# Building the graph's cell matrices with one-hots of one chunk between additions, and the gated unit's products in three rounded ones

## The chip, the cores and the metric

The program runs on one core of one Trainium2 chip. The number that counts is the device time of one execution in microseconds (us), median of several runs. The kernel is written engine by engine: TensorE (PE, with its weight loads PEld), VectorE (DVE), ScalarE (ACT), GpSimd (POOL) and SyncE (SP, which issues most of the DMAs) each have an instruction stream of their own, and they wait for each other only where the program says so, by semaphores.

## The reference

Four graph layers in a row over 1250 nodes of 512 values and 21250 edges. Each layer takes `h = relu(layernorm(x))` and adds its result to x:

```python
deg = max(segment_sum(1, dst), 1)
x = x + L0(h, ...)    # mean of the neighbours' rows, two linear maps, layernorm
x = x + L1(h, ...)    # two weighted graph convolutions, rows divided by their norm
x = x + L2(h, ...)    # messages and a gated unit, below
x = x + L3(h, ...)    # sum of the neighbours' rows by edge_weight1, one linear map

def L2(h, src, dst, edge_attr, ...):
    m = relu(concat(h[src], edge_attr) @ W1.T + b1) @ W2.T + b2
    agg = segment_sum(m, dst)
    i_r, i_z, i_n = split(agg @ W_ih.T + b_ih)
    h_r, h_z, h_n = split(h @ W_hh.T + b_hh)
    r, z = sigmoid(i_r + h_r), sigmoid(i_z + h_z)
    n = tanh(i_n + r * h_n)
    h_new = (1 - z) * n + z * h
    return h + gamma * (h_new - run_mean) * rsqrt(run_var + eps) + beta
```

Everything is float32.

## The kernel before

The 1250 nodes are 10 tiles of 128 (NT = 10), a row of 512 is 4 blocks of 128 (KT = 4). The stages, with their place in the profiled execution in us:

- **Sorting (0 to 297).** The edges are sorted on the chip by their cell (tile of the target, tile of the source: 100 cells of 128x128) into chunks of 128 edges with one cell each, 272 chunks (CELL_CHUNKS), and in a second order by target for layer 2. Indirect DMAs of POOL write the sorted records to memory. Beside it PE turns and folds the weights.
- **Building (297 to 540).** Each chunk of 128 edges becomes a part of three matrices (edge count, edge_weight, edge_weight1) over its cell. ACT makes the one-hot of the sources (`one_hot_sources`, abs at L847 and relu at L852). DVE makes the one-hot of the targets (`hots`, L1560: the row of numbers `iota1` compared with each edge's number, two chunks in one instruction, 128x256). POOL multiplies it by the two weights (`weights_turn`, L725, two chunks in one instruction, 128x512). PE multiplies the sources' one-hot with the three targets' one-hots (L1142, 128x384) into one of four banks of PSUM, and DVE adds the bank to the cell's place in SBUF (`add_block`, L1576). That place comes from a table: a TENSOR_LOAD (L1565) takes 8 places into registers of DVE's sequencer at the start of each turn of 8 chunks (TURN). The one-hots have 8 slots each. An addition waits for the one before it, as two may go to the same cell. POOL also issues one of layer 2's 168 scatters (L717) in each turn, 32 of them in this stage (EARLY = 4 groups of COL = 8).
- **Layers 0 and 1 (540 to 838).** Products with these matrices. POOL does the other 136 scatters, then clears `g` at L760 once layer 1 is done, and then waits for the first gathers.
- **Messages (838 to 1149).** For 184 chunks of 128 edges, POOL gathers rows (L784) and copies their indices four chunks at a time (L771), PE, DVE and ACT make the messages and add them up by target. SP loads the gated unit's six 512x512 matrices in 48 pieces between its other loads: 4 ahead of the loop, 4 in each turn of 16 chunks, 4 behind it.
- **The gated unit (1149 to 1372).** For each tile t, PE turns the tiles of h and of the sums by `turn_tile` (L1046; one tile ahead), ACT copies them to SBUF, and PE makes four results by `linear` (L1060): r and z with 8 blocks each, hn and in with 4 each. All of it is float32 by float32; the profile shows each such matmul as two records, so a tile has 24 matmuls and 48 records. DVE reads the banks and computes the gates from L1743 to L1769 with ACT's sigmoid, tanh and square root between; the batch-norm's factors are made once at L1723 to L1726, ahead of the first tile.
- **Layer 3 (1372 to 1487).** The sum over neighbours with three rounded products: each operand is the sum of a high part, rounded to fp32r by a copy on ACT (L992, L997), and a low part, the rest, made by a subtraction on DVE (L1732, L1737); PE adds high by high, high by low and low by high (L1328).

The four banks `pb[4..7]` go round over all of DVE's jobs in the order of a list (V), and a job may only be begun when the fourth before it has been read:

```python
def to_dve(job):
    at_least(pe, dve_read, V[job] - 3)
    return dve_bank(job)
```

## Time and profile before

| | |
|---|---|
| median of 3 runs | 1490.85 us (1489.72 to 1490.96) |
| the profiled execution | 1488.92 us, span 1486.7 us |
| mean granted clock of TensorE | 0.957 |
| PE busy | 1309.6 us, 88% of the span |
| DVE busy | 988.1 us, 66% |
| POOL busy | 719.2 us, 48% |
| PEld busy | 685.9 us, 46% |
| ACT busy | 565.0 us, 38% |
| of the chain that ended last: PE | 45% |
| issue (waiting for nothing shown) | 17% |
| POOL | 14% |
| DMA | 13% |
| DVE | 9% |

The span runs from the first to the last instruction; the execution's own time is 2.2 us longer. Busy shares are means over stages with different limits: PE is busy nearly throughout, but a matmul that PE could have made sooner counts as busy all the same. The clock granted to TensorE is 2.4 GHz at 1.00 and 1.2 GHz at 0.50. So each stage has to be read for itself, by the distance from one step to the next on the engine that is never free.

### The profile page before, as it was taken

How to read it: one execution, taken by the hardware profiler on the slowest of the kernel's cores; microseconds unless marked ns; L12 is line 12 of the kernel's file. 1: busy time of each engine (PE TensorE's matmuls, PEld its weight loads, DVE VectorE, ACT ScalarE, POOL GpSimd, SP SyncE). 2: the span in 40 equal slices, each digit the busy share in tenths (PEclk: the TensorE clock that was granted, in tenths of full speed). 3: DMA queues.
4: the chain of work that ended last, by engine and by line, in shares of the span. 5: the costliest groups of instructions: out<-in, count | busy, mean ns of one | idle time of the engine just before them, and what ended most of it. 6: DMA issues, size and time to landing. Idle time of an engine off the chain costs nothing.

```text
span 1486.7 us, 19898 instructions
## 1 busy us (share of the span) xinstructions
PE 1309.6 (88%) x4184; PEld 685.9 (46%) x4184; DVE 988.1 (66%) x1719; ACT 565.0 (38%) x1438; POOL 719.2 (48%) x873
## 2 busy tenths in 40 slices
PE   5859898098888888959998899999998999997998
PEld 2534443043333333438874444444454444443775
DVE  8798253078888889841286388888896576667432
ACT  0211311066666620121011388888886221222210
POOL 0677777677777725766771266676663000000000
PEclk9989999599999999979999999999999999998999
DMA  8832522110000044443223577777775000000220
GB/s 337 322 118 65 191 66 79 46 57 18 19 21 16 9 181 156 121 154 96 89 81 127 161 224 215 228 227 225 227 221 184 20 1 0 1 0 18 71 89 34
DMA packets 87236, 167.86 MB, mean 113 GB/s; under 512 B 16108, under 2 KB 44654, under 8 KB 84628
## 3 DMA queue, kind: packets, MB, share of 16 engines
q1 hardware_dynamic: 59044, 102.19, 20.4%
q0 software_dynamic: 25472, 59.97, 13.2%
q10 hardware_dynamic: 2672, 5.11, 1.1%
q8 instruction: 24, 0.39, 0.1%
q14 instruction: 24, 0.20, 0.0%
HBM read 115.97 MB, written 51.25 MB: 112 GB/s over the span
## 4 chain that ended last, share of the span: by engine, by line
PE 45%; issue 17%; POOL 14%; DMA 13%; DVE 9%; POOLq 1%; ACT 1%; DVEq 1%; ACTq 0%
PE pb L1060 21%; DMA arena<-p_rows,gidx 11%; POOL cell_rows L671 8%; PE pb L1142 6%; PE pb L1168 6%; PE pb L1328 5%; PE pb L1176 2%; POOL tiles L725 2%; PE pb L1046 1%; POOL arena L725 1%; PE pb L1083 1%; PE pb L1258 1%; DMA cell_rows<-tiles,gidx 1%; DVE arena L1560 1%; POOL arena L784 1%
## 5 line engine op out<-in xcount | busy, mean ns | idle before, releaser
L784 POOL DMA_INDIRECT arena<-p_rows,gidx x184 | 191.5, 1041 | 67.3 <-issue 58.4
L717 POOL DMA_INDIRECT dst_rows<-ering,gidx x168 | 172.2, 1025 | 100.0 <-issue 71.4
L671 POOL DMA_INDIRECT cell_rows<-tiles,gidx x168 | 168.8, 1004 | 68.0 <-issue 39.7
L1258 PE MATMUL pb<-arena 128*128 128x512 f32 x368 | 191.6, 604 | 5.6 <-ACT arena L944 5.6
L1576 DVE TENSOR_TENSOR arena<-pb,arena 128x384 f32 x272 | 150.0, 552 | 45.8 <-PE pb L1142 24.4
L1060 PE MATMUL pb<-ws,tiles 128*128 128x512 f32 (+1 forms) x360 | 146.3, 554 | 12.0 <-ACT tiles L806 12.0
L1684 DVE TENSOR_TENSOR arena<-pb,arena 128x512 f32<-128x512 f32 x184 | 124.4, 686 | 41.6 <-DMA arena<-p_rows,gidx 39.5
L1142 PE MATMUL pb<-arena 128*128 128x384 f32 x272 | 107.5, 520 | 47.9 <-POOL arena L725 46.1
L847 ACT ACTIVATE arena<-iota,free 128x128 f32<-128x128 f32 x272 | 94.3, 393 | 123.4 <-PE pb L1142 82.4
L1142 PE MATMUL pb<-tiles,arena 128*128 128x384 f32 x272 | 106.2, 514 | 22.8 <-POOL tiles L725 21.0
L1060 PE MATMUL pb<-arena,tiles 128*128 128x512 f32 x240 | 103.9, 593 | 0.0
L1060 PE MATMUL pb<-arena 128*128 128x512 f32 x240 | 103.8, 592 | 0.0
L1274 PE MATMUL pb<-high,low 128*128 128x512 f32 x138 | 93.7, 679 | 7.7 <-DVE arena L1699 6.3
L1060 PEld LDWEIGHTS pb<-ws,tiles 128*128 128x128 f32 x360 | 66.6, 193 | 69.0 <-issue 53.6
L1691 DVE SCALAR_TENSOR_TENSOR low<-arena,high 128x512 fp32r<-128x512 f32 x138 | 94.4, 684 | 4.4 <-ACT high L951 2.2
L951 ACT ACTIVATE high<-arena 128x512 fp32r<-128x512 f32 x138 | 86.1, 624 | 25.7 <-DVE arena L1684 21.7
L1142 PEld LDWEIGHTS pb<-arena 128*128 128x128 f32 x272 | 42.2, 192 | 113.1 <-ACT arena L852 85.3
L1168 PE MATMUL pb<-arena 128*128 128x256 f32 x400 | 88.2, 380 | 2.0 <-DVE arena L1649 1.5
L725 POOL TENSOR_TENSOR arena<-arena,free 128x512 f32<-128x512 f32 x68 | 70.8, 1042 | 35.8 <-DVE arena L1560 32.4
L1168 PEld LDWEIGHTS pb<-arena 128*128 128x128 f32 x400 | 75.8, 190 | 16.0 <-issue 3.3
L1328 PE MATMUL pb<-parts 128*128 128x512 f32 x300 | 75.2, 409 | 8.3 <-DVE parts L1737 8.2
L1176 PE MATMUL pb<-ws,arena 128*128 128x512 f32 x160 | 73.6, 616 | 9.5 <-DVE tiles L1620 7.0
(258 smaller groups left out, 2129.8 us busy)
## 6 DMA issues: line engine op xcount, KB each, us to landing
dst_rows<-arena SPq DMA_DIRECT2D x6, 2046.0 KB, 17.5
ering<-in_edge_attr_dram SPq DMA_DIRECT2D x41, 256.0 KB, 3.0
arena<-adj SPq DMA_DIRECT2D x10, 640.0 KB, 3.8
arena<-dst_rows SPq DMA_DIRECT2D x24, 264.0 KB
arena<-wt_gru SPq DMA_DIRECT2D x48, 128.0 KB
ws<-dst_rows SPq DMA_DIRECT2D x22, 264.0 KB, 2.9
arena<-in_x_dram SPq DMA_DIRECT2D x18, 256.0 KB, 8.7
arena<-in_L_gnn_W_hh_dram SPq DMA_DIRECT2D x3, 1024.0 KB
```

The costliest lines, as they stand in the source:

```text
L671: nc.gpsimd.indirect_dma_start(cell_rows[:, :], bass.IndirectOffsetOnAxis(gidx[:, SPAN * a + k:SPAN * a + k + 1], 0), cring[:, a, k], None ...
L717: nc.gpsimd.indirect_dma_start(dst_rows[:, :], bass.IndirectOffsetOnAxis(gidx[:, k:k + 1], 0), ering[:, k, :], None).then_inc(e_scattered[ ...
L725: nc.gpsimd.tensor_tensor(hot[:, :, 1:3], hot[:, :, 0:1].to_broadcast([P, 2, 2, P]), cellm[:, bass.ds(TURN * i + 2 * q, 2), 2:4].unsqueeze ...
L784: nc.gpsimd.indirect_dma_start(rows[:, k, :], None, p_rows[:, :], bass.IndirectOffsetOnAxis(gidx[:, k:k + 1], 0)).then_inc(g_landed[k], 16)
L1060: ins = nc.tensor.matmul(b[:, 0:wide], x[:, k], w[:, k], start=m == 0, stop=m == n - 1)
L1142: nc.tensor.matmul(pb[k % 4][:, 0:3 * P], ohs[:, k], ohd(k, 1).rearrange("p a m d -> p (a m d)"), start=True, stop=True).then_inc(block_do ...
L1168: ins = nc.tensor.matmul(b[:, 0:wide], blocks_of[:, s], rows_of[:, s, 0:wide], start=s == 0, stop=s == NT - 1)
L1176: ins = nc.tensor.matmul(b[:], matrix(0, t)[:, s], ws[:, s // KT, s % KT] if s < 2 * KT else h[:, s], start=s == 0, stop=s == NT - 1)
L1258: nc.tensor.matmul(e_bank(k)[:], erowT[:, k % 4], w1e_sb, start=True, stop=True).then_inc(edge_mm, 1)
L1328: ins = nc.tensor.matmul(b[:], a3[:, t % 2, left, k], h3[:, right, k], start=k == 0 and left + right == 0, stop=k == NT - 1 and left == 1)
L1576: vtt(cell, pb[k % 4][:, 0:3 * P].rearrange("p (m d) -> p m d", m=3), cell, ALU.add).then_inc(block_added, 1)
L1684: vtt(row, e_bank(k)[:], row, ALU.add).then_inc(msg_added, 1)
```

## The change

Two parts, made together.

**Building.** DVE makes the one-hot of one chunk (128x128) between every two additions, 8 chunks ahead, rather than of two chunks at every second; the row of numbers it compares with lies in PSUM (`counting`, a copy of `iota1` in `pb[4]`). POOL weights four chunks in one instruction (HALF = 4, 128x1024). DVE's turn is 16 chunks; of the places it loads 1 at its start and 3 more after each third addition. A scatter goes out every 16 chunks, so 16 lie in this stage (EARLY = 2) and 152 behind it.

**The gated unit.** Its operands are split as in layer 3. At its start ACT rounds the 24 blocks of the six matrices (`high_of_weights`) and DVE makes their low parts (`low_of_weights`). For each tile the high part is copied by ACT out of the bank in which PE turned it, and the low part made there by DVE (`low_of_turned`), for h and for the sums; there is one set of these parts, written anew for each tile. A result is three fp32r products for each block. PE first does the parts of r, z and hn that come from h, then the parts of r, z and in that come from the sums, and DVE reads hn, r, z, in. The batch-norm's factors come behind the weights' low parts. The pieces of the matrices are loaded 8 ahead of the message loop and none behind it; layer 3's first matrices and its weight are loaded when hn of the last tile is there.

```diff
@@ building, POOL
             def weights_turn(i, with_column=None):
-                for q in range(TURN // 2):
-                    pool.wait_ge(dst_hot, TURN // 2 * i + q + 1)
+                for q in range(2):
+                    pool.wait_ge(dst_hot, TURN * i + HALF * (q + 1))
...
-                    if q == 1 and with_column is not None:
-                        scatter_column(with_column)
+                if with_column is not None:
+                    scatter_column(with_column)
...
-                    weights_turn(COL * i + k, k)
+                    weights_turn(2 * COL * i + 2 * k, k)
+                    weights_turn(2 * COL * i + 2 * k + 1)
@@ building, DVE
-            def hots(i, q):
-
-                at_least(dve, block_done, TURN * i + 2 * q - 6)
-                vtt(ohd(2 * q, 2)[:, :, 0], iota1[:].unsqueeze(1).to_broadcast([P, 2, P]),
-                    cellm[:, bass.ds(TURN * i + 2 * q, 2), 1:2].to_broadcast([P, 2, P]), ALU.is_equal).then_inc(dst_hot, 1)
+            def hot(i, k):
+
+                vtt(ohd(k % TURN, 1)[:, :, 0], counting.unsqueeze(1),
+                    cellm[:, bass.ds(2 * TURN * i + k, 1), 1:2].to_broadcast([P, 1, P]), ALU.is_equal).then_inc(dst_hot, 1)
...
             def turn(i, last):
-                at = table_values(cell_at[0:1, bass.ds(TURN * i, TURN)], (CELLS - 1) * P)
-                for q in range(TURN // 2):
-                    add_block(i, 2 * q, at[2 * q])
-                    if not last or q < TURN // 2 - 3:
-                        hots(i + (q + 3) // 4, (q + 3) % 4)
-                    add_block(i, 2 * q + 1, at[2 * q + 1])
+                at = list(table_values(cell_at[0:1, bass.ds(2 * TURN * i, 1)], (CELLS - 1) * P))
+                for k in range(2 * TURN):
+                    add_block(i, k, at[k])
+                    if k % 3 == 0 and len(at) < 2 * TURN:
+                        at += table_values(cell_at[0:1, bass.ds(2 * TURN * i + k + 1, 3)], (CELLS - 1) * P)
+                    if not last or k < TURN:
+                        hot(i, k + TURN)
@@ the gated unit, SP
-            for n in range(4):
+            whole = DST_CHUNKS // WIDE
+            first_pieces = GRU_PIECES - 4 * (whole - 1)
+            for n in range(first_pieces):
                 gru_piece(n)
...
-            for n in range(4 * whole, GRU_PIECES):
-                gru_piece(n)
...
-            sp.dma_start(ws[:, 0].rearrange("p k f -> p (k f)"), wt_dram["w3"]).then_inc(w3_loaded, 16)
-            sp.wait_ge(sums_added, DST_PAIRS)
+            sp.wait_ge(for_dve, V[("hn", NT - 1)] + 1)
@@ the gated unit, ACT
+            def high_of_turned(kind, t):
+
+                if t:
+                    act.wait_ge(for_dve, V[("hn" if kind == "hgT" else "in", t - 1)] + 1)
+                act.wait_ge(part_turned, 2 * t + (1 if kind == "hgT" else 2))
+                nc.scalar.copy(high[:, 0 if kind == "hgT" else 2], part_bank(kind, t)[:]).then_inc(part_high, 1)
+
+            def high_of_weights(b):
+                for k in range(KT):
+                    nc.scalar.copy(gru_high[b][k], gru_w[:, b, k]).then_inc(weight_high, 1)
@@ the gated unit, PE
+            def three_products(t, job, parts, b, first, last):
+
+                bank = to_dve((job, t)) if first else dve_bank((job, t))
+                for k in range(KT):
+                    if t == 0:
+                        pe.wait_ge(weight_low, KT * b + k + 1)
+                    high_w, low_w = gru_high[b][k], gru_low[b][:, k]
+                    nc.tensor.matmul(bank[:], parts[0][:, k], high_w, start=first and k == 0, stop=False)
+                    nc.tensor.matmul(bank[:], parts[0][:, k], low_w, start=False, stop=False)
+                    ins = nc.tensor.matmul(bank[:], parts[1][:, k], high_w, start=False, stop=last and k == KT - 1)
+                if last:
+                    ins.then_inc(for_dve, 1)
...
-                pe.wait_ge(act_read, A[("hgT", t)] + 1)
-                hg, at = blocks4(hgT[t % 2]), blocks4(r2T[t % 2])
-                linear(("r", t), [(hg, gru_w[:, 3]), (at, gru_w[:, 0])], D)
-                linear(("z", t), [(hg, gru_w[:, 4]), (at, gru_w[:, 1])], D)
-                linear(("hn", t), [(hg, gru_w[:, 5])], D)
-                linear(("in", t), [(at, gru_w[:, 2])], D)
+                pe.wait_ge(part_low, 2 * t + 1)
+                three_products(t, "r", hg_parts, 0, True, False)
+                three_products(t, "z", hg_parts, 1, True, False)
+                three_products(t, "hn", hg_parts, 2, True, True)
+                pe.wait_ge(part_low, 2 * t + 2)
+                three_products(t, "r", at_parts, 3, False, True)
+                three_products(t, "z", at_parts, 4, False, True)
+                three_products(t, "in", at_parts, 5, True, True)
@@ the gated unit, DVE
+            def low_of_turned(kind, t):
+
+                n = 0 if kind == "hgT" else 1
+                dve.wait_ge(part_high, 2 * t + n + 1)
+                vtt(high[:, 2 * n + 1], part_bank(kind, t)[:], high[:, 2 * n].bitcast(F32), ALU.subtract).then_inc(part_low, 1)
...
+                read(("hn", t), lambda b: vtt(n, b[:], bw_v, ALU.add))
+                if t + 1 < NT:
+                    low_of_turned("hgT", t + 1)
                 for gate, name, c_v, b_v in ((r, "r", cr_v, bx_v), (z, "z", cz_v, by_v)):
                     read((name, t), lambda b: vstt(gate, c_v, count, b[:], ALU.mult, ALU.add))
                     vtt(gate, gate, b_v, ALU.add).then_inc(gate_in, 1)
-                read(("hn", t), lambda b: vtt(n, b[:], bw_v, ALU.add))
...
                 vtt(n, n, m, ALU.add).then_inc(gate_in, 1)
+                if t + 1 < NT:
+                    low_of_turned("r2T", t + 1)
```

```order
L1565 TENSOR_LOAD places_at
L1573 REGISTER_ALU
L1576 ISA [waits block_added,block_done]
L1576 TENSOR_TENSOR arena<-pb,arena 128x3x128
L1560 ISA [waits block_done]
L1560 TENSOR_TENSOR tiles<-iota,free 128x2x128
L1573 REGISTER_ALU
L1576 ISA [waits block_added,block_done]
L1576 TENSOR_TENSOR arena<-pb,arena 128x3x128
L1573 REGISTER_ALU
L1576 ISA [waits block_added,block_done]
L1576 TENSOR_TENSOR arena<-pb,arena 128x3x128
```

And the same place now (L1637 the additions, L1621 the one-hots):

```order
L1626 TENSOR_LOAD places_at
L1634 REGISTER_ALU
L1637 ISA [waits block_added,block_done]
L1637 TENSOR_TENSOR arena<-pb,arena 128x3x128
L1626 ISA
L1626 TENSOR_LOAD places_at
L1621 ISA
L1621 TENSOR_TENSOR arena<-pb,free 128x128
L1634 REGISTER_ALU
L1637 ISA [waits block_added,block_done]
L1637 TENSOR_TENSOR arena<-pb,arena 128x3x128
L1621 ISA
```

Every addition now has a one-hot behind it, the one-hot reads `pb` in place of `iota`, and a load of places stands between an addition and its one-hot at every third chunk.

The second place is DVE in a tile of the gated unit, before (L1743 and L1744 are r and then z, L1745 is hn):

```order
L1743 SCALAR_TENSOR_TENSOR arena<-arena,deg,pb 128x512 [waits for_dve]
L1744 TENSOR_TENSOR arena<-arena 128x512 [waits dve_read]
L1745 TENSOR_TENSOR arena<-pb,arena 128x512 [waits for_dve]
L1747 TENSOR_TENSOR arena<-arena 128x512 [waits gate_out,dve_read]
L1750 TENSOR_TENSOR arena<-arena,free 128x512 [waits gate_out,step]
```

And now (L1821 is hn, L1790 the low part of the next tile's h, L1825 and L1826 r and z):

```order
L1821 TENSOR_TENSOR arena<-pb,arena 128x512 [waits for_dve]
L1790 TENSOR_TENSOR high<-pb,high 128x512 [waits part_high,dve_read]
L1825 SCALAR_TENSOR_TENSOR arena<-arena,deg,pb 128x512 [waits for_dve]
L1826 TENSOR_TENSOR arena<-arena 128x512 [waits dve_read]
L1825 SCALAR_TENSOR_TENSOR arena<-arena,deg,pb 128x512 [waits for_dve]
L1826 TENSOR_TENSOR arena<-arena 128x512 [waits dve_read]
L1828 TENSOR_TENSOR arena<-arena 128x512 [waits gate_out]
```

hn is read first, and a subtraction is put between it and r. The other one stands later in the tile, behind the sum for n and ahead of the wait for the tanh:

```order
L1840 TENSOR_TENSOR arena<-arena 128x512 [waits step]
L1790 TENSOR_TENSOR high<-pb,high 128x512 [waits part_high]
L1846 TENSOR_TENSOR arena<-arena 128x512 [waits gate_out]
L1847 TENSOR_TENSOR arena<-arena 128x512 [waits step]
L1567 BN_STATS stats<-arena 128x6 [waits step]
```

What moved: in place of two waits for the gates' banks ahead of hn there are two more subtractions, one between bank reads and one where DVE waited for ACT.

## Rows read from the trace of the kernel before

**Rows 1.** Stretches: us, busy (instructions) by engine, granted clock, DMA share, GB/s.
```profile
297.00:540.00 243.00, 213.44 (x544) 83.06 (x544) 198.24 (x405) 148.59 (x402) 177.50 (x184) 0.99 0.07 22
1127.70:1134.00 6.30, 5.67 (x9) 2.53 (x10) 5.68 (x10) 3.95 (x11) 2.55 (x3) 0.52 0.38 105
1150.00:1360.00 210.00, 210.00 (x546) 97.02 (x545) 134.36 (x215) 54.25 (x78) 0.00 (x0) 1.00 0.02 7
```

**Rows 2.** Timeline, DVE, building: start us, us, engine line operation [idle before <-releaser].
```profile
406.04 0.56 DVE L1576 TENSOR_TENSOR arena<-pb,arena 128x384 f32 x1 [0.63 <-PE pb L1142]
...
532.16 0.56 DVE L1576 TENSOR_TENSOR arena<-pb,arena 128x384 f32 x1 [0.20 <-DVE arena L1576]
532.63 0.41 DVE L1560 TENSOR_TENSOR tiles<-iota,free 128x256 f32<-128x256 f32 x1
532.97 0.55 DVE L1576 TENSOR_TENSOR arena<-pb,arena 128x384 f32 x1
```

**Rows 3.** Groups by form, building, DVE's one-hots into `tiles`: count | busy, mean ns | idle before.
```profile
L1560 DVE TENSOR_TENSOR tiles<-iota,free 128x256 f32<-128x256 f32 x67 | 37.6, 562 | 0.0
```

**Rows 4.** Instructions on the table of places: duration ns min/median/max.
```profile
L1565 DVEq TENSOR_LOAD <-places_at x126: 300/308/865, 295.0 to 1146.9; - x126
```

**Rows 5.** Timeline, building: DVE, POOL, PE.
```profile
402.89 0.45 DVE L1560 TENSOR_TENSOR arena<-iota,free 128x256 f32<-128x256 f32 x1
...
403.61 1.04 POOL L725 TENSOR_TENSOR arena<-arena,free 128x512 f32<-128x512 f32 x1 [0.56 <-DVE arena L1560]
405.84 1.05 POOL L725 TENSOR_TENSOR tiles<-tiles,free 128x512 f32<-128x512 f32 x1
...
407.04 3.18 PE L1142 MATMUL pb<-tiles,arena 128*128 128x384 f32 x8 [0.67 <-POOL tiles L725]
```

**Rows 6.** POOL's scatters (group), and its clearing of `g` (timeline).
```profile
L717 POOL DMA_INDIRECT dst_rows<-ering,gidx x168 | 172.2, 1025 | 100.0 <-issue 71.4 <-POOL gidx L705 27.1 <-DMA ering<-in_edge_attr_dram 1.2
...
804.05 4.37 POOL L760 MEMSET arena<- 128x5120 f32 x1 [19.99 <-DVE arena L1668]
```

**Rows 7.** Timeline, POOL, end of the message loop: index copies.
```profile
1112.68 0.18 POOL L771 COPY gidx<-ws 128x4 int32<-128x4 int32 x1 [0.29 <-DMA arena<-p_rows,gidx]
1121.21 0.18 POOL L771 COPY gidx<-arena 128x4 int32<-128x4 int32 x1 [2.53 <-DMA arena<-p_rows,gidx]
1130.16 0.18 POOL L771 COPY gidx<-arena 128x4 int32<-128x4 int32 x1 [3.28 <-DMA arena<-p_rows,gidx]
```

**Rows 8.** Timeline, PE, a tile of the gated unit.
```profile
1237.20 20.77 PE L1060 MATMUL pb<-arena,tiles 128*128 128x512 f32 x48
1258.68 3.60 PE L1060 MATMUL pb<-arena 128*128 128x512 f32 x8
```

**Rows 9.** The chain of waits, layer 3's sum: start us, us, what.
```profile
1400.23 6.85 PE pb L1328 x30
```

**Rows 10.** Timeline, start of layer 3: high parts, low parts, PE.
```profile
1369.66 2.16 ACT L997 CAST parts<-arena 128x512 fp32r<-128x512 f32 x4
1371.85 2.50 DVE L1737 TENSOR_TENSOR parts<-arena,parts 128x512 fp32r<-128x512 f32 x4
1372.68 16.40 PE L1328 MATMUL pb<-parts 128*128 128x512 f32 x60 [8.21 <-DVE parts L1737]
```

**Rows 11.** Timeline, DVE, the batch-norm's factors: first and last.
```profile
1149.10 0.42 DVE L1723 TENSOR_SCALAR vec<-vec 128x512 f32<-128x512 f32 x1
1155.06 0.69 DVE L1726 TENSOR_TENSOR free<-free,vec 128x512 f32<-128x512 f32 x1
```

**Rows 12.** Timeline, DVE, gated unit: from hn to the sum for n, last tile.
```profile
1361.08 0.69 DVE L1745 TENSOR_TENSOR arena<-pb,arena 128x512 f32<-128x512 f32 x1 [1.96 <-PE pb L1060]
1368.39 0.69 DVE L1759 TENSOR_TENSOR arena<-arena 128x512 f32<-128x512 f32 x1
```

**Rows 13.** Timeline, DVE, gated unit: from the tanh to the next tile's r.
```profile
1263.27 0.69 DVE L1763 TENSOR_TENSOR arena<-arena 128x512 f32<-128x512 f32 x1 [0.69 <-ACT arena L1010]
1267.22 0.74 DVE L1743 SCALAR_TENSOR_TENSOR arena<-arena,deg,pb 128x512 f32<-128x512 f32 x1
```

More of the change, by code:

```diff
@@ L66 @@
 TURN = 8
[L67 removed]
+HALF = TURN // 2
+EARLY = CELL_CHUNKS // TURN // (2 * COL)
 def at_least(eng, semaphore, value):
@@ L120, in build_gnn, with sb_behind @@
         a3 = parts3[:, 2 * NT * D:].rearrange("p (b a s d) -> p b a s d", b=2, a=2, s=NT)
+        def sb_behind(words, name, shape, dt):
+            with nc.sbuf_tensor(name + "_before", [P, words], F32):
+                return sb_under(name, shape, dt)
+        gru_low = [sb_behind(low.shape[1] + b * KT * D, f"gru_low{b}", [P, KT, D], F32R) for b in range(6)]
+        over_rows = low.shape[1] + 6 * KT * D + 4 * D
+        spare_high = sb_behind(over_rows, "spare_high", [P, 9, D], F32R)
         arena = sb("arena", [P, 2 * AW + 3 * NT * D])
@@ L282, in build_gnn @@
         h2T = rows[:, 0:2].rearrange("p b (k n) -> p b k n", k=KT)
-        hgT = [tiles[:, 1], rows[:, 4]]
-        r2T = [tiles[:, 0], rows[:, 5]]
+        acur[0] = 2 * AW - 8 * D
         vec2_start = acur[0]
@@ L384, in build_gnn @@
         act_jobs += [("h2T", t) for t in range(NT)]
-        act_jobs += [(kind, t) for t in range(NT) for kind in ("r2T", "hgT")]
         act_jobs += [("agg3T", t) for t in range(NT)]
@@ L742, in _ @@
                 weights_and_edges(i)
-            for i in range(COL * EARLY, CELL_CHUNKS // TURN):
+            for i in range(2 * COL * EARLY, CELL_CHUNKS // TURN):
                 weights_turn(i)
@@ L997, in high_rows @@
                 nc.scalar.copy(h3[:, 0, k], h[:, k]).then_inc(high3, 1)
-            copies(0)
+            act.wait_ge(gru_loaded, 16 * GRU_PIECES)
+            act.wait_ge(summed, DST_CHUNKS)
+            high_of_turned("hgT", 0)
+            high_of_weights(0)
+            high_of_turned("r2T", 0)
+            for b in range(1, 6):
+                high_of_weights(b)
+            root("bn", vec[:, 1])
             for t in range(NT):
                 if t + 1 < NT:
-                    copies(t + 1)
+                    high_of_turned("hgT", t + 1)
                 for k in range(2):
```

73 lines of the change are left out of this document (50 added, 23 removed).

## The prediction, made before the changed kernel was run

> **What bounds the kernel now.** I read the busy time by stretch first, then the timelines of the two stages that the change touches, then the end of the stage between them.
>
> The building stage takes 243 us for 272 chunks, and no engine is busy all of it: PE 213, DVE 198, POOL 178 [rows 1]. So it is a cycle, and I looked for the engine whose steps set the distance. That is DVE. An addition lasts 0.56 us and the next one starts 0.20 behind its end, 0.76 from start to start; with a one-hot between, the one-hot starts 0.47 behind the addition and the next addition 0.34 behind that, 0.81 in all [rows 2]. A turn of 8 is then 4 x 0.76 + 4 x 0.81 = 6.3, and its first addition waits 0.63 in place of 0.20 [rows 2]; the profile names PE there, but the load of eight places takes up to 0.865 [rows 4], more than the rest of an addition can hide. That makes 6.7. The stretch has some 3 us of start in it, so a turn takes 240 / 34 = 7.1; the rest is one-hots that last 562 ns on the mean instead of 410 [rows 2, 3].
>
> The gated unit is bound by PE: busy 210.0 of 210.0 at granted clock 1.00, DVE only 134 [rows 1]. A tile is 21.48 us from start to start, 48 records at 0.429 = 20.6 and the turning of two tiles, 0.9 [rows 8].
>
> **Building, part by part.** The one-hot of 128 rather than 256 columns should be shorter by the difference of columns at the additions' rate: (0.56 - 0.41) us for (384 - 256) columns is 0.15 for 128, so 0.27 [rows 2]. It starts 0.47 behind the addition, and the next addition could start 0.34 - 0.15 = 0.19 behind it, at 0.66. But the wait on the addition before holds it to 0.76. So all sixteen additions of a turn are 0.76 apart, 12.2 us, and the one-hots cost nothing: the 0.20 wait covers them, and without that cover each would cost some 0.3.
>
> The loads: 92 of the 126 are of one place and 34 of eight; with a shortest of 300 ns and a longest of 865, three places are 0.30 + 2 x 0.08 = 0.46 [rows 4]. That fits in the 0.47 before the one-hot, but there are also the sequencer's two small instructions. From below such a load costs nothing; from above, if it cost what one of eight does, the one-hot would start at 0.9 and the addition at 1.1, 0.34 late. I take 0.05, five times a turn, as its duration is near the lower one. The first load of a turn, one place, and the branch: 0.25. Sum 12.7 for 16.
>
> A page speaks against these loads: the Trainium skill, Runtime: NRT & Kernel Launch, Instruction fetch mechanics, has about 200 ns for each register loaded. By it eight would take 1.6 us, and the trace has 0.865 [rows 4], so the rule doesn't hold for this table. By it three would take 0.6, and the stage would be some 12 us longer than in my sum.
>
> **POOL** gets one instruction of 1024 in place of two of 512 at 1.04 [rows 5]: 2.08, or a little less. I take 2.08, as nothing shows that an instruction has a fixed part worth counting; the lower end is 1.9. The group of four chunks waits for its fourth one-hot. The chain: four one-hots are there 3 x 0.76 + 0.47 + 0.27 = 3.0 after the first of four additions; POOL starts 0.27 later (403.61 against 402.89 + 0.45), works 2.08, PE starts 0.15 later (407.04 against 406.89) [rows 5], and I allow 0.9 for the matmul and its way to DVE, two records at the 0.40 from one to the next (3.18 for 8) and a little. That is 6.4 for eight chunks, 12.8 for sixteen: just over DVE's 12.7. The scatter, 1.03 [rows 6], comes once in sixteen chunks and may push a group by 0.1 to 0.2. So 13.0 a turn, 17 turns, 221, with the 3 us of start 224 **against 243: -19**. Ends: 12.4 a turn, 214; and 12.2 + 0.4 + 5 x 0.34 = 14.3, 246.
>
> Why the row of numbers in PSUM counts: one-hots are stretched (562 against 410) while additions, which read one operand from PSUM, keep to 0.55 to 0.56 [rows 2, 3]. A rule bears on this: the Trainium skill, SBUF — State Buffer, Who interferes with whom, says that a DVE instruction with two SBUF inputs contends with a GpSimd instruction that reads SBUF, and one with a single SBUF input does not. By it the new one-hot never stretches; if it didn't hold, a stretch of 0.15 would add 0.07 a chunk beyond the 0.10 of slack in 0.76, some 15 us.
>
> **What moves with it.** Sixteen scatters go behind the stage. A scatter costs POOL (172.2 + 100.0) / 168 = 1.62 us, together 26 [rows 6]. POOL begins them 19 earlier, so it ends 7 later against the rest of the program; it had 20.0 us of idle time before it clears `g` only where layer 1 sets the moment, and that moment is 19 earlier too. 20 - 26 leaves the clearing 6 late. `g` is needed only when the messages' sums begin, 30 us on. Cost nothing.
>
> **Between the stages.** The four last pieces of the matrices and layer 3's loads leave the end of the message loop. There POOL's index copies wait 2.53 and 3.28 us for gathers in place of 0.29 [rows 7], and PE falls to a granted clock of 0.52 for 6.3 us after it [rows 1]. I take back 5 us. Four pieces more ahead of the loop, 0.5 MB, may delay the first gathers by 1. Together **-4** (ends 0 and -7).
>
> **The gated unit.** A rounded product: 30 in 6.85 us, 0.228 each [rows 9]. A tile has 24 x 3 = 72 of them, 16.4, and the turning 0.9: 17.3 against 21.5. DVE's tile: from hn to the end of the sum for n 8.0 [rows 12]; r and z 3.0 (0.74 + 0.69 and a gap of 0.04 behind each, twice); from the tanh to the next tile 3.95 [rows 13]; two low parts at 0.68, the second lying in the 0.69 of waiting for ACT [rows 13]. 8.0 + 3.0 + 0.7 + 0.7 + 3.95 = 16.4. So PE stays the bound, by 0.9 us. Round trips: the sums' low part of the next tile is ready 12.4 behind hn's read, PE wants it 17.3 behind hn; the low part of h is ready 1.4 behind, PE wants it after 9.1. Both are hidden. r and z now come when hn is done, at 2.7 and 5.5 us, so DVE waits some 0.9 for z and runs 1.7 us behind PE, at PE's pace.
>
> The start is new. DVE makes 24 low parts at 0.62 (four in 2.50), ACT the high ones at 0.54 (four in 2.16) [rows 10], with two parts of the first tile: DVE is done 17.6 us after 1149.1, when it has ended the messages' sums. Then the factors, 6.65 (1149.10 to 1155.75) [rows 11], which lay beside PE before and now lie on the path. Tile 0's gates begin at 24.4, tile 1's h part is ready at 25.8. PE did tile 0 at DVE's pace, is done by 19, and waits 6 to 7 us; the granted clock may fall to 1.2 GHz, as it did around 1127.7 [rows 1], and 3 us of work are lost in a stretch that waits anyway. Tile 1's sum part needs its low part at 24.4 + 12.4 = 36.8; with the slow clock PE gets there at 37.2. From then 17.3 a tile: tile 9's at 175.7. From there DVE ends the sum for n 14.3 later (5.5 to z, then 1.5 and 7.3), and PE starts layer 3 another 3.6 later, as before (1372.68 against 1369.08) [rows 10, 12]. Sum 193.6, against 1372.7 - 1149.1 = 223.6: **-30**. Layer 3's three loads start at 175.7 and have 18 us.
>
> **Sum.** -19 - 4 - 30 = -53 on the profiled execution's 1488.9: 1435.9. The median shown is 1.9 above that execution, so **1438**.
>
> **Rivals.**
> 1. *Loads of places block DVE's sequencer.* For: six loads in sixteen chunks against two, each just ahead of an instruction that can't pass it. Against: 308 ns is the usual duration [rows 4]. If three cost what eight do, the stage takes 246: 1460. The page's 200 ns a register would give 1438 + 12 = 1450, an in-between of it.
> 2. *DVE becomes the bound of the gated unit.* It has 0.9 us to spare of 17.3. If copies on ACT wait behind a table load or a sigmoid, 2.5 us more a tile make 18.9: 9 x 1.6 = 14, so 1452.
> 3. *It does more.* Building at 214 and 7 from the message loop: 1425.
> 4. *The one-hots don't gain,* because the stage hangs on POOL's group of four: 2.08 late by a scatter each time. 14 a turn, 241: 1455.
> 5. *Slower: PE's clock in the gated unit.* DVE and PE are now close; if DVE's chain leaves PE resting in every tile, the granted clock falls and stays at 1.2 GHz, where a tile takes 34.6. Nine tiles at that are 156 us more: 1594. It decides once more than 5.9 us a tile are lost, about 12 us of each at the lower clock. Against: the clock was low for 6.3 us only [rows 1], and my chain has no rest of PE in a tile.
>
> **How the numbers follow.** My forecast 0.52; rival 1 0.15; rival 2 0.13; rival 3 0.09; rival 4 0.07; rival 5 0.02; and 0.02 that both parts give back what they win, near 1490. Only the last two aren't faster. The unknown costs of the forecast itself are -8 to +12. The range 1418 to 1463 takes in rivals 1 to 4 and leaves out rival 5, the last case and the tails. A measurement of this kernel can tell 0.2%, 3 us. Faster 0.96, same 0.01, slower 0.03.
>
> **What would show it.** Additions 0.76 apart with a one-hot of 0.27 to 0.30 between each two, a turn of 13 us; loads of three near 0.46; POOL's instruction 2.0 to 2.1; PE in the gated unit 17.3 a tile and never idle after tile 1; 6 us of idle PE once at its start, and a low granted clock there; index copies at the end of the message loop waiting 0.3. I am wrong on the first part if one-hots follow a load by more than 0.1 late or PE waits for POOL's four; on the second if PE waits for a low part in later tiles.

## The result, and the profile after

| | before | after |
|---|---|---|
| median | 1490.41 us (4 runs, 1489.72 to 1490.96) | 1480.04 us (4 runs, 1475.42 to 1483.11) |
| ratio | | 0.9928 [0.9901, 0.9955] |
| the profiled execution | 1488.92 us | 1475.42 us |
| TensorE's mean granted clock | 0.957 | 0.946 |

The change is 10 us faster (the ratio is of the means, with its 95% interval), where 53 were forecast, and the time lies above the range of 1418 to 1463. The profiled execution is the shortest of its four, so the two profiles are 13 apart and the medians 10. The page after, busy time and the chain:

```profile
PE 1261.4 (86%) x4424; PEld 753.7 (51%) x4424; DVE 1025.0 (70%) x1900; ACT 578.2 (39%) x1462; POOL 703.0 (48%) x805
...
PE 38%; issue 15%; DMA 14%; DVE 13%; POOL 12%; DVEq 5%; POOLq 1%; ACT 1%; ACTq 0%; SPq 0%
```

New in the chain is DVEq, DVE's sequencer, with 5%. By stages, this profile against that of before (us):

| stage | before | after | difference | forecast |
|---|---|---|---|---|
| start of the span to the last addition of building (539.6, 559.7) | 539.6 | 559.7 | +20 | -19 |
| from there to the first index copy of the message loop (838.9, 858.0) | 299.3 | 298.3 | -1 | 0 |
| message loop: DVE done with the sums at 1149.1 and 1168.25 | 310.2 | 310.3 | 0 | -4 |
| gated unit, to the first matmul of layer 3's sum (1372.68, 1359.68) | 223.6 | 191.4 | -32 | -30 |
| layer 3, to the end of the span | 114.0 | 114.0 | 0 | 0 |

So one part did what was forecast and the other the contrary. Here is the stretch of building (columns as in [rows 1]), and then the loads of places in it, with their duration in ns as min/median/max, as in [rows 4]:

```profile
297.00:557.00 260.00, 205.91 (x540) 105.38 (x541) 204.57 (x532) 148.40 (x402) 145.35 (x92) 0.94 0.04 13
```
```profile
L1626 DVEq TENSOR_LOAD <-places_at x100: 309/745/890, 299.8 to 554.3; - x100
```

A load of three takes 745 ns, not the 460 of my estimate; 13 of the 85 take 840 to 890, which I can't explain. DVE's timeline in the middle of the stage, for [rows 2]:

```profile
398.44 0.55 DVE L1637 TENSOR_TENSOR arena<-pb,arena 128x384 f32 x1
398.91 0.28 DVE L1621 TENSOR_TENSOR tiles<-pb,free 128x128 f32<-128x128 f32 x1
399.19 0.56 DVE L1637 TENSOR_TENSOR arena<-pb,arena 128x384 f32 x1
...
399.95 0.56 DVE L1637 TENSOR_TENSOR arena<-pb,arena 128x384 f32 x1
400.96 0.29 DVE L1621 TENSOR_TENSOR arena<-pb,free 128x128 f32<-128x128 f32 x1 [0.45 <-issue]
401.17 0.55 DVE L1637 TENSOR_TENSOR arena<-pb,arena 128x384 f32 x1
```

Without a load, a one-hot starts 0.47 behind the addition and the next addition 0.76 (398.44, 398.91, 399.19). Behind the addition at 399.95 stands a load, and the one-hot comes at 1.01, the next addition at 1.22: 0.46 late. Five such loads are 2.3 us a turn of 16, 39 in 17 turns. The forecast of -19 had 4 us for them, so with them as measured it is -19 - 4 + 39 = +16 of the +20 seen. Behind the thirteen long loads the next addition is 0.65 late, which makes it +18. The chain in this stretch names the loads themselves:

```profile
407.26 0.75 DVEq L1626
...
410.07 0.87 DVEq L1626
```

PE now rests up to 1.9 us for POOL's group of four, which waits for its late one-hots. The granted clock falls to 0.50 at 399.0, 1.1 us after such a rest has ended, and is back at 1.00 by 402.5; behind the stage's start there are 14 rests of over 1.5 us in it and eight such dips of 3.4 us. Eight records (four matmuls) take 4.42 us here and 2.85 a little later.

```profile
397.86 4.42 PE L1177 MATMUL pb<-arena 128*128 128x384 f32 x8 [1.88 <-POOL arena L745]
...
405.30 2.85 PE L1177 MATMUL pb<-arena 128*128 128x384 f32 x8 [0.32 <-POOL arena L745]
```

POOL's instruction of 1024 is 1.90 (forecast 2.08):

```profile
L745 POOL TENSOR_TENSOR arena<-arena,free 128x1024 f32<-128x1024 f32 x34 | 64.5, 1897 | 60.2 <-DVE arena L1621 59.3
```

The end of the message loop still has a long wait of an index copy, one in place of two ([rows 7]):

```profile
1133.86 0.18 POOL L792 COPY gidx<-ws 128x4 int32<-128x4 int32 x1 [0.39 <-DMA arena<-p_rows,gidx]
1143.96 0.18 POOL L792 COPY gidx<-arena 128x4 int32<-128x4 int32 x1 [4.16 <-DMA arena<-p_rows,gidx]
1150.54 0.18 POOL L792 COPY gidx<-arena 128x4 int32<-128x4 int32 x1 [0.85 <-DMA arena<-p_rows,gidx]
```

In the gated unit PE has one long wait, at tile 1, for a bank that DVE reads late because it makes the factors first. PE runs slowly for 3 us after it, at a granted clock of 0.50 (0.42 us from matmul to matmul, then 0.23):

```profile
1194.25 0.74 PE L1361 MATMUL pb<-ws_high,high 128*128 128x512 f32 x1 [5.33 <-DVE arena L1825]
1194.79 0.63 PE L1362 MATMUL pb<-gru_low,high 128*128 128x512 f32 x1
1195.21 0.63 PE L1363 MATMUL pb<-ws_high,high 128*128 128x512 f32 x1
...
1198.21 0.40 PE L1362 MATMUL pb<-gru_low,high 128*128 128x512 f32 x1
1198.45 0.39 PE L1363 MATMUL pb<-ws_high,high 128*128 128x512 f32 x1
```

hn is read for the first tile at 1192.04 and for the last at 1344.34: 16.9 a tile, where [rows 8] has 21.5. The first three distances are 16.2, at DVE's pace, and the last six 17.3, at PE's.

### The profile page after: what moved, and what is told of

The parts are those of the page before. It is cut to its first block, busy times and chain, and to the rows that moved or that the text cites. A ratio compares the mean times of both kernels' runs of the same rounds, so it can differ in the third digit from the quotient of the medians.

```text
span 1473.7 us, 20196 instructions
## 1 busy us (share of the span) xinstructions
PE 1261.4 (86%) x4424; PEld 753.7 (51%) x4424; DVE 1025.0 (70%) x1900; ACT 578.2 (39%) x1462; POOL 703.0 (48%) x805
## 4 chain that ended last, share of the span: by engine, by line
PE 38%; issue 15%; DMA 14%; DVE 13%; POOL 12%; DVEq 5%; POOLq 1%; ACT 1%; ACTq 0%; SPq 0%
DMA arena<-p_rows,gidx 10%; POOL cell_rows L691 8%; PE pb L1094 7%; PE pb L1203 6%; PE pb L1390 5%; PE pb L1177 4%; PE pb L1361 3%; PE pb L1363 3%; PE pb L1362 3%; DVEq L1626 3%; DMA cell_rows<-tiles,gidx 3%; PE pb L1211 2%; DVE arena L1637 2%; PE pb L1293 1%; POOL arena L805 1%
## 5 line engine op out<-in xcount | busy, mean ns | idle before, releaser
L737 POOL DMA_INDIRECT dst_rows<-ering,gidx x168 | 166.4, 990 | 105.8 <-issue 72.4
L1293 PE MATMUL pb<-arena 128*128 128x512 f32 x368 | 191.3, 603 | 4.1 <-ACT arena L965 4.1
L1177 PE MATMUL pb<-arena 128*128 128x384 f32 x272 | 112.0, 562 | 80.6 <-POOL arena L745 80.5
L1637 DVE TENSOR_TENSOR arena<-pb,arena 128x384 f32 x272 | 151.5, 557 | 19.0 <-PE pb L1177 15.8
L1177 PEld LDWEIGHTS pb<-arena 128*128 128x128 f32 x272 | 54.8, 211 | 134.6 <-POOL arena L745 57.8
L1177 PE MATMUL pb<-tiles,arena 128*128 128x384 f32 x272 | 97.1, 500 | 15.6 <-POOL tiles L745 15.6
L972 ACT ACTIVATE high<-arena 128x512 fp32r<-128x512 f32 x138 | 86.1, 624 | 25.6 <-DVE arena L1748 21.5
L1362 PE MATMUL pb<-gru_low,high 128*128 128x512 f32 x240 | 94.1, 392 | 0.0
L745 POOL TENSOR_TENSOR arena<-arena,free 128x1024 f32<-128x1024 f32 x34 | 64.5, 1897 | 60.2 <-DVE arena L1621 59.3
L745 POOL TENSOR_TENSOR tiles<-tiles,free 128x1024 f32<-128x1024 f32 x34 | 64.6, 1901 | 51.8 <-DVE tiles L1621 51.8
L1203 PEld LDWEIGHTS pb<-arena 128*128 128x128 f32 x400 | 75.8, 190 | 16.0 <-issue 3.3
L1177 PEld LDWEIGHTS pb<-tiles,arena 128*128 128x128 f32 x272 | 51.2, 195 | 63.2 <-POOL tiles L745 32.7
```

What stands on the lines that cost most here:

```text
L737: nc.gpsimd.indirect_dma_start(dst_rows[:, :], bass.IndirectOffsetOnAxis(gidx[:, k:k + 1], 0), ering[:, k, :], None).then_inc(e_scattered[ ...
L745: nc.gpsimd.tensor_tensor(hot[:, :, 1:3], hot[:, :, 0:1].to_broadcast([P, HALF, 2, P]), cellm[:, bass.ds(TURN * i + HALF * q, HALF), 2:4]. ...
L1177: nc.tensor.matmul(pb[k % 4][:, 0:3 * P], ohs[:, k], ohd(k, 1).rearrange("p a m d -> p (a m d)"), start=True, stop=True).then_inc(block_do ...
L1203: ins = nc.tensor.matmul(b[:, 0:wide], blocks_of[:, s], rows_of[:, s, 0:wide], start=s == 0, stop=s == NT - 1)
L1293: nc.tensor.matmul(e_bank(k)[:], erowT[:, k % 4], w1e_sb, start=True, stop=True).then_inc(edge_mm, 1)
L1362: nc.tensor.matmul(bank[:], parts[0][:, k], low_w, start=False, stop=False)
```

## The experiments

My theory after the result was that the loads of three block DVE's sequencer, and that this alone is the loss. Its rivals were the group of four on POOL, the row of numbers in PSUM, and a clash of the two parts.

**Each part alone.** `unit_only` is the changed kernel with the building part of the diff taken back, `building_only` the kernel before with that part alone; of each the first line stands here.

```diff
@@ unit_only, the changed kernel with the earlier weights_turn, hots, turn and EARLY
-            def hot(i, k):
+            def hots(i, q):
@@ building_only, the kernel before with the new ones
-            def hots(i, q):
+            def hot(i, k):
```

> The building stage as before, the gated unit (and its loads) as changed. Theory A (the stages add up; the building stage alone gave the gain back): building stage 240 us from its first matmul to its last addition, from there as in the changed kernel; the gated unit 191 to 192 us against 223.5, so the whole is 31 to 35 us under before: 1456 to 1460. Theory B (the stages interact, for example by the scatters moved behind the building stage, and part of the lost time lies elsewhere): gain under 25 us, over 1465.

Measured: 1457.32 (4 runs, 1454.3 to 1458.95) against 1491.39, ratio 0.9774 [0.9738, 0.9809]: -34, as theory A says.

> The building stage as changed, the gated unit as before. Theory A: slower than before by the 19 us that the two traces differ by in that stage, 1507 to 1512, and more spread from run to run than before. Theory B: within 10 us of before.

Measured: 1506.46 (5 runs, 1504.3 to 1508.8), ratio 1.0093 [1.0065, 1.0121]: +15, a little under A's range and beyond B's. Its runs don't scatter more than those of the kernel before. Its loads of places are the same:

```profile
L1567 DVEq TENSOR_LOAD <-places_at x100: 308/745/891, 302.2 to 555.5; - x100
```

In the profiles the parts don't clash. Against the kernel before, the gated unit takes 32 us less with and without the new building stage, and building takes 20 more with the new unit and 18 more without. The whole profiled executions give -34.6 and +19.9, together -14.7 where both at once gave -13.5. The medians give -34 and +15, together -19 where both at once gave -10. Those 8.6 us aren't explained: runs of the kernel before reach from 1487 to 1497 in these comparisons, but a loss of this size that only some executions have when both parts are in is not ruled out.

**The loads.** In `loads_of_eight` the places come eight at a time, at the turn's start and after the eighth addition.

```diff
-                at = list(table_values(cell_at[0:1, bass.ds(2 * TURN * i, 1)], (CELLS - 1) * P))
+                at = list(table_values(cell_at[0:1, bass.ds(2 * TURN * i, TURN)], (CELLS - 1) * P))
...
-                    if k % 3 == 0 and len(at) < 2 * TURN:
-                        at += table_values(cell_at[0:1, bass.ds(2 * TURN * i + k + 1, 3)], (CELLS - 1) * P)
+                    if k == TURN - 1:
+                        at = at + list(table_values(cell_at[0:1, bass.ds(2 * TURN * i + TURN, TURN)], (CELLS - 1) * P))
```

> The changed kernel, but the places are loaded eight at a time, twice in a turn of 16, instead of 1 and five times 3. Theory L (each load of three holds DVE's sequencer 0.745 us between an addition and its one-hot, so the next addition comes 0.47 late, five times a turn): loads of eight last 0.60 as before; additions behind one come 1.1 apart, twice a turn, the others 0.76; a turn 12.9 to 13.3, the stage 222 to 230 us instead of 259, granted clock 0.98 or more, the whole near 1445. Theory P (POOL's groups of four hold the stage, the loads lie in their shadow): PE still waits for POOL and the stage stays over 245.

Measured: 1443.6 (one run). The last addition starts at 527.0 in place of 559.7:

```profile
L1637 DVE TENSOR_TENSOR arena<-pb,arena x272: 551/558/560, 299.7 to 527.0; 128x384 f32 x136
```
```profile
L1626 DVEq TENSOR_LOAD <-places_at x32: 594/598/617, 306.1 to 514.4; - x32
```

Eight places take 0.60, less than three. Theory L holds: 227 us from the first addition to the last and 1.08 behind a load, as the lines around the load in the middle of a turn show:

```profile
413.26 0.56 DVE L1637 TENSOR_TENSOR arena<-pb,arena 128x384 f32 x1
414.13 0.29 DVE L1621 TENSOR_TENSOR tiles<-pb,free 128x128 f32<-128x128 f32 x1 [0.30 <-issue]
414.34 0.55 DVE L1637 TENSOR_TENSOR arena<-pb,arena 128x384 f32 x1
```

One edit gives back 33 of the 39 us; the load in the middle still costs 0.32 a turn, 5 in all. A turn is now about 13.45: sixteen additions at 0.76, that 0.32, and waits of 0.24 and 0.79 for PE, the second at the turn's start. PE's rests of 1.9 us are gone (1.0 at most) and its clock in the stage is 0.99. This edit alone doesn't tell the loads' own delay from the fallen clock; the run of sizes off the fours below does.

**Which sizes are dear.** `load_sizes` takes 1, 1, 2, 4 and 8 places, `sizes_off_the_fours` 1, 4, 5 and 6, `loads_of_one` sixteen times one, each ahead of its addition.

```diff
@@ load_sizes (sizes_off_the_fours: {0: 4, 4: 5, 9: 6})
-                    if k % 3 == 0 and len(at) < 2 * TURN:
-                        at += table_values(cell_at[0:1, bass.ds(2 * TURN * i + k + 1, 3)], (CELLS - 1) * P)
+                    more = {0: 1, 1: 2, 3: 4, 7: 8}.get(k, 0)
+                    if more:
+                        at += table_values(cell_at[0:1, bass.ds(2 * TURN * i + k + 1, more)], (CELLS - 1) * P)
@@ loads_of_one
-                at = list(table_values(cell_at[0:1, bass.ds(2 * TURN * i, 1)], (CELLS - 1) * P))
                 for k in range(2 * TURN):
-                    add_block(i, k, at[k])
+                    at = table_values(cell_at[0:1, bass.ds(2 * TURN * i + k, 1)], (CELLS - 1) * P)
+                    add_block(i, k, at[0])
```

> The changed kernel, but the places of a turn of 16 are loaded 1, 1, 2, 4 and 8 at a time: a measurement of what a load costs by its number of places. Theory N (time grows with the number): 1 about 0.31, 2 about 0.38, 4 about 0.8, 8 at 0.6 would contradict it. Theory W (an odd or uneven number of places is what is dear): 1 at 0.31, 2, 4 and 8 all under or at 0.6, and only the three of the changed kernel at 0.745. The stage takes 225 to 240 us by either.

> In the building part the places are loaded in sizes 1, 4, 5 and 6, starting at places 0, 1, 5 and 10 of the turn (the four no longer starts at a multiple of four). Measured so far, each at a multiple of its own size: one 0.31 us, two 0.53, four 0.35, eight 0.60; three, at places 1, 4, 7, 10 and 13, 0.745. Theory F, a load takes 0.1 us and 0.22 for each register, or 0.25 for four at once: four 0.35, five 0.57, six 0.79, wherever they start. Theory G, four at once needs a start at a multiple of four: four 1.0, five 1.2, six 1.4. Theory H, only a power of two is quick: four 0.35, five and six over 0.8, five no shorter than six. Time: F 1450, G 1475.

> The building part takes one place in front of each addition, 16 loads of one in a turn of 16 in place of 1 and five of three; everything else is the changed kernel. Loads of one took 304 to 312 ns in the run with mixed sizes, and there the one behind a turn's first addition brought the next one-hot 0.12 us late (0.59 behind the addition in place of 0.47). Theory A, the cost goes by how long a load lasts beyond the time DVE's sequencer has to spare: 16 x 0.1 a turn at most, so the stage takes some 17 x (12.2 + 1.6 + 0.8) = 248 + 3 of start, about 10 us less than the changed kernel's 262; 1470, and with 0 for a load 1445. Theory B, each load costs a fixed amount (the 0.46 us measured for a load of three, whatever its size), so sixteen cost more than six: 17 x 16 x 0.46 = 125 against 39, about 1560.

Measured, one run each: 1445.64, 1479.89 and 1448.17. These are loads of two, four and eight in one turn of `load_sizes`, and then of four, five and six, which start at places 1, 5 and 10, in `sizes_off_the_fours` (the one of six is from the turn before):

```profile
L1626 DVEq TENSOR_LOAD <-places_at x1: 532/532/532, 409.7 to 409.7; - x1
...
L1626 DVEq TENSOR_LOAD <-places_at x1: 351/351/351, 411.6 to 411.6; - x1
...
L1626 DVEq TENSOR_LOAD <-places_at x1: 600/600/600, 414.7 to 414.7; - x1
```
```profile
L1626 DVEq TENSOR_LOAD <-places_at x1: 966/966/966, 408.5 to 408.5; - x1
...
L1626 DVEq TENSOR_LOAD <-places_at x1: 1184/1184/1184, 412.3 to 412.3; - x1
...
L1626 DVEq TENSOR_LOAD <-places_at x1: 1401/1401/1401, 401.6 to 401.6; - x1
```

The DVE timeline of `load_sizes` around its load of two:

```profile
409.64 0.56 DVE L1637 TENSOR_TENSOR arena<-pb,arena 128x384 f32 x1
410.44 0.29 DVE L1621 TENSOR_TENSOR arena<-pb,free 128x128 f32<-128x128 f32 x1 [0.25 <-issue]
410.72 0.56 DVE L1637 TENSOR_TENSOR arena<-pb,arena 128x384 f32 x1
```

From such rows, duration and distance from the addition ahead to the one-hot behind (0.47 without a load):

| places, the first one | duration, us | addition to one-hot, us |
|---|---|---|
| 1 | 0.313 | 0.59 |
| 2, at 2 | 0.532 | 0.80 |
| 3, at 1, 4, 7, ... | 0.745 | 1.01 |
| 4, at 1 | 0.966 | 1.24 |
| 5, at 5 | 1.184 | 1.46 |
| 6, at 10 | 1.401 | 1.66 |
| 4, at 4 | 0.351 | 0.62 |
| 8, at 8 | 0.600 | 0.86 |

Theory N falls by the four at place 4 (0.351, and it said 0.8). Theory W fits `load_sizes`, but it falls with theories F and H by the four at place 1 (0.966). Theory G holds within 0.03 us (it said 1.0, 1.2, 1.4), and its time of 1475 is 5 short. Each place more costs 0.22, except that four which start at a multiple of four cost 0.25 together after the first 0.10. Starts off the fours were 1, 5 and 10 for these sizes. The runs don't vary the registers that a load fills apart from its place in the table, so which of the two has to be aligned is open.

The second column is the first plus 0.26 to 0.28 in every row: in this place, between an addition and its one-hot, a load is hidden for its first 0.2 us only, and all beyond that makes the one-hot late. `loads_of_one` has its loads elsewhere, behind the one-hot and ahead of the addition, where DVE waits for the addition before anyway. There a load of 0.30 costs 0.02: additions are 0.78 apart. The fixed cost per load of theory B is refuted: sixteen loads of one end the stage at 527.8, as loads of eight do.

`sizes_off_the_fours` also tells the loads from the fallen clock. Its stage is as long as that of the change (301.0 to 560.8), with PE's rests 1.4 us at most and a granted clock of 1.00:

```profile
301.00:560.80 259.80, 194.26 (x542) 94.76 (x541) 205.88 (x536) 146.53 (x396) 142.61 (x90) 1.00 0.03 9
```

So loads that last too long are enough for the loss, without a low clock. They make the additions 2.8 us late a turn there and 2.4 in the changed kernel, so a small share of the clock in the latter is not ruled out.

The Trainium skill, Runtime: NRT & Kernel Launch, Instruction fetch mechanics, has some 200 ns for each register, of loads from HBM. These runs, with the table in SBUF, show 0.22 for each, which is near it, but 0.25 for a whole group of four at a multiple of four.

**The row of numbers.** `row_in_sbuf` is `loads_of_eight` with the one-hots reading SBUF.

```diff
-            counting = pb[4][:, 0:P]
-            link(nc.vector.tensor_copy(counting, iota1[:]))
+            counting = iota1[:]
```

> The version with loads of eight (1443.6, one run), with the one-hots' row of numbers read from SBUF again and not from PSUM. Theory P (the prediction's): with both operands in SBUF the one-hot is stretched while POOL works, which is 7.6 us of a turn of 13.4: from 0.28 to some 0.43 for about half of them; 0.07 a chunk at most beyond the slack of 0.10, so between 0 and 15 us longer, 1444 to 1459. Theory Q: the row's place does not matter, one-hots stay at 0.27 to 0.29 and the time at 1443.6 within 3.

Measured: 1522.45 (one run), 79 more: Q is refuted, and P's 15 at most was too small by five times. The timeline, POOL and DVE:

```profile
404.69 0.56 DVE L1637 TENSOR_TENSOR arena<-pb,arena 128x384 f32 x1
404.87 1.90 POOL L745 TENSOR_TENSOR arena<-arena,free 128x1024 f32<-128x1024 f32 x1 [2.51 <-DVE arena L1621]
405.17 1.75 DVE L1621 TENSOR_TENSOR tiles<-iota,free 128x128 f32<-128x128 f32 x1
```

The one-hot begins 0.3 after POOL's instruction and ends 0.15 behind its end (406.77, 406.92); the one-hots after it take 0.28 again. It isn't stretched in proportion, it is held until POOL is done: 65 of the 264 one-hots that start behind 300 take over 0.5 us, each of them ends 0.15 behind the end of a POOL instruction, and none of the others overlaps one. And since the next group of four needs that one-hot, POOL then rests 2.5 us. The kernel before has the same in small, which I had read as a stretch ([rows 3]): 41 of its one-hots take over 0.5 us, and each ends 0.29 behind a POOL instruction.

```profile
409.43 1.04 POOL L725 TENSOR_TENSOR arena<-arena,free 128x512 f32<-128x512 f32 x1 [0.47 <-POOL gidx L705]
409.94 0.82 DVE L1560 TENSOR_TENSOR arena<-iota,free 128x256 f32<-128x256 f32 x1
```

The Trainium skill, SBUF — State Buffer, Who interferes with whom, calls the shared port an exclusive lock, and these rows agree.

**POOL by twos.** `weights_by_twos` is `loads_of_eight` with two chunks to an instruction.

```diff
-HALF = TURN // 2
+HALF = 2
...
-                for q in range(2):
+                for q in range(TURN // HALF):
```

> The version with loads of eight (1443.6, one run), with POOL's weighting two chunks at a time as in the kernel before: eight instructions of 512 elements at 1.04 us in a turn of 16, in place of four of 1024 at 1.90. Theory C: the group of four holds the turn (in the version with loads of eight PE waits 37 times for POOL, 26 us in all, and DVE's additions wait 0.24 and 0.5 to 0.8 for PE in a turn of 13.45). By twos those waits fall by some 0.5 a turn: 12.9 a turn, 9 us less, 1435. Theory D: POOL's busy time rises by 0.7 a turn and the number of its instructions doubles, while DVE's chain is the bound anyway; no change or up to 5 us more, 1443 to 1449.

Measured: 1449.58 (one run). From 300 to 522 PE waits for POOL once, and for DVE 30 times (us in total, times, longest); with loads of eight it waited 26 us for POOL, in 37 waits:

```profile
PE pb L1177 <- DVE arena L1637: 15.3, 30, 0.8
PE pb L1177 <- POOL tiles L745: 0.8, 1, 0.8
```

The stage is 4 shorter (298.4 to 522.0 against 299.7 to 527.0), half of what C said, and the stages from there to the message loop took 8 more. The time of this one run is at the upper end of D's and decides nothing. So with loads of eight the group of four is a small cost, and not what broke the forecast.

**The end of the message loop, and the best version.** In `eight_and_rows_later` SP issues its three broadcast loads of rows only behind the loop; `twos_and_rows_later` has twos as well. `loads_of_eight_timed` is `loads_of_eight` again, with the time taken beside them.

```diff
             sp.wait_ge(vec_folded, 1)
+            sp.wait_ge(sums_added, DST_PAIRS)
             sp.dma_start(vec[:, 0], mean2.rearrange("(a f) -> a f", a=1).to_broadcast([P, D])).then_inc(vec2_loaded, 16)
```

> The version with loads of eight again, now timed: of places, DVE loads eight at the turn's start and eight after the eighth addition. One run gave 1443.6, and the change as it was made has 1480.0. If the loads of three are the whole loss, it is 1438 to 1447, and its runs scatter less than those of the change (1475 to 1483), as PE no longer rests 1.9 us at a time in the building stage.

> Loads of eight, and SyncE's three loads of rows (mean, variance, bias; each spread over 128 partitions) wait for the end of the messages' sums; before, they are issued in the last turn of the message loop, and in all five profiles looked at a gather's index copy waits 3.4 to 4.2 us for a load of records right behind them. Theory R, these rows hold up the last records: the wait falls to 0.5 and the whole is 3 shorter than with loads of eight alone, which is timed beside it. Theory S, the wait is due to SyncE itself, which issues that last load of records only when a buffer is free (its issue takes 6.5 us in the trace): the wait stays and the time is that of loads of eight within 1.

> As the run before, and POOL weights two chunks at a time. In the single look at twos the building stage took 223.6 us (298.4 to 522.0) against 227.3 with fours, but the stages from there to the message loop 307.0 against 298.7. Theory T, the 4 us won in building are real and the other 8 are a chance of that run: 4 less than the version with fours timed beside it. Theory U, layers 0 and 1 lose it again each time: 3 to 6 more than with fours.

| | median (4 runs each) | ratio to before (1490.93) |
|---|---|---|
| loads_of_eight_timed | 1443.05 (1440.31 to 1444.38) | 0.9668 [0.9638, 0.9699] |
| eight_and_rows_later | 1441.34 (1438.23 to 1443.97) | 0.9664 [0.9635, 0.9693] |
| twos_and_rows_later | 1441.37 (1437.44 to 1446.97) | 0.9664 [0.9625, 0.9703] |

The index copies, with loads of eight and then with the rows later as well:

```profile
1109.04 0.19 POOL L792 COPY gidx<-arena 128x4 int32<-128x4 int32 x1 [3.78 <-DMA arena<-p_rows,gidx]
```
```profile
1104.80 0.18 POOL L793 COPY gidx<-arena 128x4 int32<-128x4 int32 x1 [0.41 <-DMA arena<-p_rows,gidx]
```

Theory R holds in the profile: both start their message loops at 824.9, the copy is 4.2 earlier, and the first matmul of layer 3's sum 3.9 (1326.0, 1322.1). The medians differ by 1.7 with runs that scatter over 4 to 6, so the time alone doesn't show it. The 6.5 us that S was built on are a row of two issues of 0.36 with the wait for a buffer between them (6.49 and 6.45 us in all). It is there in both runs, which speaks against S.

Twos: building ends at 522.8 in place of 526.1, and the median is the same. In the profile the stages from there to the message loop take 302.9 against 298.7, so the 3 us won are lost again there, as U says and as in the single run before; why isn't known, and the times scatter too much (10 us) to choose between T and U. Nothing shows that loads of eight scatter less: their runs span 4.1 us against 7.7 of the change, but those of `building_only`, which has the loads of three too, span only 4.5.

## Why the prediction was wrong

- **Loads of places: the step that failed.** I wrote "three places are 0.30 + 2 x 0.08 = 0.46 [rows 4]. That fits in the 0.47 before the one-hot", and took 0.05 each. Three errors lie in it. The 865 ns from which I had 0.08 a place is one single load at 295.0; the other 33 loads of eight in [rows 4] take 0.60. The cost isn't a line through the sizes one and eight at all: eight go in groups of four, three don't, at 0.22 a place. And the gap of 0.47 isn't free time for the sequencer; some 0.2 of it is. Measured: 0.745 for a load and 0.46 late for the next addition, 2.3 us a turn in place of 0.25. That is 39 us where I had 4, so 35 of the 43 by which the gain fell short.
- **The bound from above.** My bound, 0.34 late "if it cost what one of eight does", took eight as dearer than three, and so wasn't a bound. Rival 1 had the mechanism, with 246 us for the stage; it took 263. I had set aside the 200 ns a register of the Trainium skill (Runtime: NRT & Kernel Launch, Instruction fetch mechanics), since eight take less than 1.6 us. It was nearer the truth for three than my 0.46 (0.6 by it, 0.745 measured), but the 12 us that I added for it were too few, as I had taken the hidden part too large.
- **The rest of building was nearly right.** With the forecast in brackets: one-hots took 0.28 (0.27), additions were 0.76 apart, and with loads of eight a turn took 13.45 (13.0) and the stage 230 us (224). POOL's 1024 took 1.90 and not 2.08. PE waited for it all the same, 53 us in the stage, about half of it since the loads made its one-hots late: with loads of eight 26 us of such waits stayed. Rival 4, the group of four, is worth 3 to 4 us of the stage there.
- **The row in PSUM** I called worth up to 15 us; it is worth 79 in this form. The direction was right; the step that was wrong is the stretch of 0.15, as a one-hot is held for the rest of a POOL instruction that has become 1.9 long.
- **The message loop: 0 in place of -4.** I named the pieces of matrices and layer 3's loads as the cause of the waits in [rows 7]. They went away, and one wait of 3.4 to 4.2 stayed. It went with the three broadcast rows, which the change had left where they were.
- **The gated unit was right**: -32 by the profile for -30. With the forecast in brackets: a product took 0.227 (0.228), PE's one long wait 5.3 (6 to 7) with a low clock behind it, a tile 17.3 once PE was the bound (17.3), and DVE waited 1.03 for z in tiles 3 to 8 (0.9). Rivals 2 and 5 didn't come.
- **Sum:** +20 - 1 + 0 - 32 makes -13, as the profiled executions show (1488.92, 1475.42). With the loads alone mended the time is 1443, inside the range and 5 above the 1438 forecast. By the profile that is 6 more in building and 3 more in the message loop, less 2 in the gated unit and 1 between the stages.

## What to carry to other kernels

A load into a sequencer's registers between two short instructions has a price: count its duration beyond the little that is hidden (0.2 us here, between an addition and a one-hot), and read that duration for the very size and start that you will use. In these runs the cheap ones are four or eight at a multiple of four, or one in a place where the engine waits anyway. A line through the shortest and the longest row is no estimate when the row gives only min, median and max over mixed sizes: read each size by itself first. And when a step is made longer on POOL, look for DVE instructions with two SBUF operands beside it, since each can be held for all of it.

## What the runs showed of the hardware

- A TENSOR_LOAD of three registers (0.745 us) is dearer than one of eight (0.600), and four cost 0.351 or 0.966 by where they start.
- DVE's one-hot with both operands in SBUF took up to 1.99 us, held by a first POOL instruction of 2.07 (up to 1.84 by those of 1.90); with one operand in PSUM its longest was 0.292:

```profile
L1621 DVE TENSOR_TENSOR tiles<-iota,free x136: 273/282/1993, 296.5 to 598.3; 128x128 f32<-128x128 f32 x136
```
```profile
L1621 DVE TENSOR_TENSOR tiles<-pb,free x136: 280/280/292, 295.1 to 521.2; 128x128 f32<-128x128 f32 x136
```

- With rests of PE of 1.9 us in the building stage the granted clock in it was 0.94. It was 0.99 or 1.00 where the longest rest was 1.0 (`loads_of_eight`), 1.4 (`sizes_off_the_fours`) or 1.8 (`row_in_sbuf`).
- With three small broadcast loads (128 partitions from one row each) issued behind the last load of records, an index copy of POOL waited 3.78 us; with them issued later it waited 0.41.
